# Expert pairs planned one segment early, weights shared by two tiles in three buffers, and start-up transfers in the order of their use

## The reference, cut to what matters

```
mod = (silu(c) @ wmod).reshape(4, 6, 1, -1)
sa, ca, ga, sb, cb, gb = mod[:, 0], ..., mod[:, 5]
ga = (2 * (ga >= 0) - 1) * maximum(abs(ga), 0.25)     # gb the same way
h = layernorm(x) * (1 + ca) + sa
x = x + ga * attention(h)
h = layernorm(x) * (1 + cb) + sb
x = x + gb * ffn(h)
```

```
h = gelu(tokens @ W1[e] + b1[e]);  out[e] = h @ W2[e] + b2[e]
out = weight_1 * out[first expert] + weight_2 * out[second expert]
```

## Time and profile before

| | |
|---|---|
| median of 3 runs | 3398.45 us (3397.02 to 3399.81) |
| the profiled execution's own time | 3402.84 us |
| its span, first to last instruction | 3401.1 us |
| mean granted TensorE clock | 0.832 |
| PE / DVE / ACT / POOL busy | 77% / 52% / 35% / 18% |
| HBM traffic | 211.41 MB read, 53.76 MB written |

### The profile page before, as it was taken

How to read it: one execution, slowest core, us unless ns; L and a number is a source line. 1 busy time by engine, 2 the same in 40 slices (tenths; PEclk the granted TensorE clock), 3 DMA queues, 4 the chain that set the end, 5 groups by cost and what they waited for, 6 DMA issues and landing times.

```text
span 3401.1 us, 78002 instructions
## 1 busy us (share of the span) xinstructions
PE 2615.6 (77%) x33890; PEld 1936.5 (57%) x33890; DVE 1759.1 (52%) x3974; ACT 1202.0 (35%) x2396; POOL 609.8 (18%) x621
## 2 busy tenths in 40 slices
PE   3458878877896888788787969886687646779998
PEld 3244556456645655575466456555544546668887
DVE  4554766485658556765856585566439421111111
ACT  0322454255326333642553263335125412212221
POOL 0003300600060034006100600340010011102222
PEclk8667987888697979768986979797688768889999
DMA  2122201411130132013112301320110067667665
GB/s 78 32 64 57 51 2 55 103 20 45 49 77 9 45 76 57 2 46 100 33 45 50 76 9 45 75 51 2 57 63 2 7 206 235 207 232 213 199 202 152
DMA packets 230150, 266.00 MB, mean 78 GB/s; under 512 B 148064, under 2 KB 175600, under 8 KB 227440
## 3 DMA queue, kind: packets, MB, share of 16 engines
q1 hardware_dynamic: 214464, 234.79, 24.0%
q0 software_dynamic: 15344, 26.22, 3.2%
HBM read 211.41 MB, written 53.76 MB: 78 GB/s over the span
## 4 chain that ended last, share of the span: by engine, by line
PE 57%; DVE 19%; ACT 9%; DMA 7%; issue 5%; SPq 2%; POOL 0%; DVEq 0%; ACTq 0%
PE banks L1964 19%; DMA arena<-in_cols 6%; PE banks L2489 6%; PE banks L2508 4%; PE banks L2279 4%; PE banks L2196 3%; PE banks L2299 2%; PE banks L2304 2%; DVE hT L1530 2%; PE banks L2231 2%; PE banks L2066 1%; PE banks L2038 1%; PE banks L2107 1%; ACT arena L895 1%; ACT ring L895 1%
## 5 line engine op out<-in xcount | busy, mean ns | idle before, releaser
L2489 PE MATMUL banks<-arena 128*128 128x256 f32 (+1 forms) x1472 | 282.8, 357 | 88.3 <-DMA arena<-in_cols 88.2
L1873 POOL DMA_INDIRECT h_d<-h_tok,pos_now x64 | 66.0, 1031 | 1453.4 <-DVE pos_now L1715 1436.4
L2489 PEld LDWEIGHTS banks<-arena 128*128 128x128 f32 x1472 | 252.0, 213 | 120.0 <-DMA arena<-in_cols 98.0
L1082 ACT ACTIVATE arena<-banks,arena 128x256 f32<-128x256 f32 (+1 forms) x368 | 136.3, 421 | 520.3 <-PE banks L2489 520.3
L1964 PE MATMUL banks<-hT,ring 128*128 128x512 f32 x640 | 297.8, 622 | 7.8 <-DVE arena L1380 7.8
L2279 PE MATMUL banks<-arena 32*32 32x64 f32 (+2 forms) x6144 | 185.6, 294 | 144.5 <-ACT arena L906 64.5
L2279 PEld LDWEIGHTS banks<-arena 32*32 32x32 f32 (+2 forms) x6144 | 165.0, 175 | 182.2 <-issue 103.3
L2508 PE MATMUL banks<-arena 128*128 128x256 f32 x1136 | 252.6, 379 | 0.0
L2279 PE MATMUL banks<-arena,xn 32*32 32x64 f32 (+2 forms) x6144 | 166.3, 289 | 109.8 <-DVE xn L1538 58.6
L1964 PE MATMUL banks<-arena,ring 128*128 128x512 f32 x512 | 224.0, 595 | 6.2 <-ACT arena L852 6.2
L2508 PEld LDWEIGHTS banks<-arena 128*128 128x128 f32 x1136 | 212.4, 190 | 27.1
(11 more groups left out here) (364 smaller groups left out, 4827.6 us busy)
## 6 DMA issues: line engine op xcount, KB each, us to landing
arena<-in_w_ring SPq DMA_DIRECT2D x92, 1024.0 KB, 7.3
ring<-in_w_ring SPq DMA_DIRECT2D x104, 512.0 KB, 4.3
arena<-h_d SPq DMA_DIRECT2D x25, 516.0 KB, 4.0
n_d<-NA SPq DMA_DIRECT2D x8, 1024.0 KB, 3.9
arena<-n_d SPq DMA_DIRECT2D x16, 512.0 KB, 8.1
u_d<-arena SPq DMA_DIRECT2D x8, 1024.0 KB, 3.9
NA<-u_d SPq DMA_DIRECT2D x32, 256.0 KB, 5.6
arena<-in_b SPq DMA_DIRECT2D x46, 128.0 KB, 8.0
```

Source lines behind the costliest of these rows:

```text
L1082: ins_ = act.activation(hid1[:, i % 2, t, 0:SPAN[i] * P], bank[pair][:, half * T1:half * T1 + SPAN[i] * P], ACT.Gelu, bias=b1[:, i % 2, t: ...
L2489: i_ = mm(bank[t // 2][:, (t % 2) * T1:(t % 2) * T1 + n], w1[:, i % 2, t // 4, at_:at_ + P], h_cols[:, i % 2, k, 0:n], start=(k == 0), sto ...
```

## The change

Four things change together.

1. **Start-up in order of use.** SP issues the condition vector, the part of `wmod` for the first shift and scale, and `x` first, then what turn -2 needs, then the rest of `wmod`, then everything else; four semaphores (`first_in`, `pre_in`, `mod_in`, `tables_in`) take the place of one, and `started` is gone. The gates and columns, still the same products, are made inside turn -2, between the projections; the small tables inside turn -1. Gate tiles share banks (`MOD_BANK`), so three of the eight products wait for DVE to have read an earlier one (`gates_ok`).
2. **Pairs.** The expert stage still has 46 tiles, but the lists are 9 pairs of 512 rows (two full tiles that load their weights once), 7 single full tiles and 21 halves: 37 groups with loads of their own. `AFTER` mixes the halves between the pairs and singles; three full tiles end the list, behind the copy to the output.
3. **Early pairs.** Seven pairs are certain to be filled by the first seven segments alone. They are planned in turn 7 (`plan_ahead`), and the first two tiles' transposes, first products and gelu are done in turn 7. The other lists are planned behind it (`plan_rest`, on DVE within tile 0).
4. **Three buffers.** Weights have three buffers (`WBUF`), taken from arrays that are free by then.

```diff
-SEQ = [FULLS + n for n in range(HALVES)] + list(range(FULLS))
+LISTS = ((EARLY1, 2 * T1), (TWICE - EARLY1, 2 * T1), (SINGLE, T1), (HALVES, P))
+AFTER = (0, 0, 2, 2, 2, 2, 3, 3, 3, 1, 1, 1, 1, 0, 0, 0)
+TILES = [(g, part) for g, slot in enumerate(GROUPS) for part in range(2 if slot < TWICE else 1)]
+WBUF = 3
...
+            sp.dma_start(c_cols, ins["c_cols"]).then_inc(*up16(first_in))
+            sp.dma_start(wmod[0][:, :, 0:2 * D], ins["wmod"][0][:, :, 0:2 * D]).then_inc(*up16(first_in))
+            sp.dma_start(X_next, x_seg[0:1].rearrange("a p b d -> (a p) b d")).then_inc(*up16(x_next_in))
+            sp.dma_start(consts[:, 0:m0], ins["consts"][:, 0:m0]).then_inc(*up16(pre_in))
+            for t, name in ((w_qkv, "w_qkv"), (cols, "cols"), (w_beta, "w_beta")):
+                sp.dma_start(t[:], ins[name]).then_inc(*up16(pre_in))
+            sp.dma_start(wmod[0][:, :, 2 * D:], ins["wmod"][0][:, :, 2 * D:]).then_inc(*up16(mod_in))
+            sp.dma_start(wmod[1], ins["wmod"][1]).then_inc(*up16(mod_in))
...
+                if rest and not nxt:
+                    sp.wait_ge(plan_ok.handle, 1)
+                    sp.wait_ge(h_out.handle, h_out.base(seg))
+                    load_w1(0)
+                    for i in range(2):
+                        load_rows(i)
+                    load_w2(0)
...
-            sp.wait_ge(started.handle, 4 * TURNS + 4)
+            for g in range(1, WBUF):
+                load_w1(g)
+                if g == 1:
+                    for i in range(2, ROWBUF):
+                        load_rows(i)
+                load_w2(g)
+            sp.wait_ge(plan_ok.handle, 2)
             sp.wait_ge(h_out.handle, h_out.base(NSEG))
...
+            for i, (g, _) in enumerate(TILES):
+                if i:
                     sp.wait_ge(y_ok.handle, i)
+                if i + ROWBUF - 1 == SPAN.index(1):
+                    sp.wait_ge(zero_out.handle, 16 * (E1 + 1))
+                if i and i + ROWBUF - 1 < NTILES:
+                    load_rows(i + ROWBUF - 1)
+                if i and ENDS[i - 1] and TILES[i - 1][0] + WBUF < TILES1:
+                    load_w2(TILES[i - 1][0] + WBUF)
...
+                if ENDS[i] and g + WBUF < TILES1:
                     sp.wait_ge(hid1_ok.handle, 4 * (i + 1))
+                    load_w1(g + WBUF)
...
                     if pre:
                         next_norm()
+                    if not nxt:
+                        plan_ahead()
                     for hg in range(HG):
                         state_step(hg)
                     residual(2, (0, 1), 1, 0, "b_out")
+                    if not nxt:
+                        for i in range(2):
+                            columns(i)
                     layer_norm(3)
...
                 if rest:
                     norm_root(3)
+                    if not nxt:
+                        gelu_tile(0)
...
                 if rest:
                     norm_modulate(3, 1, 2)
+                    if not nxt:
+                        gelu_tile(1)
```

More of the change, by code:

```diff
@@ new lines, in plan_rest @@
+            def plan_rest():
+                plan_step(dve.tensor_copy(pad_i[0:1, :], next_row[0:1, :]))
+                plan_step(dve.memset(zeros, 0.0))
+                plan_step(dve.tensor_scalar(zeros[:, TOKEN:TOKEN + 1].bitcast(I32), token_no[:, 0:1], float(B * L), None, ALU.add))
+                plan_step(dve.scalar_tensor_tensor(left, begin, -1.0, next_row[:, :], ALU.mult, ALU.add))
+                plan_step(dve.memset(jump, float(E1 * REGION)))
+                slot = LISTS[0][0]
+                for (n, size), most in zip(LISTS[1:], MOST[1:]):
+                    assign(slot, n, size, most)
+                    slot += n
+                dve.sem_inc(*up(plan_ok))
@@ L1881, in turn @@
                 counted(seg, [zeroed, sub_step] if nxt or not rest else [zeroed])
-                if nxt or not rest:
-                    pool.sem_inc(started.handle, 1)
             turns(turn)
@@ new lines, in hidden @@
+            def hidden(i):
+                n = SPAN[i] * P
+                g = TILES[i][0]
+                pe.wait_ge(w1_in[g % WBUF].handle, 32 * (g // WBUF + 1))
+                pe.wait_ge(cols_ok.handle, i + 1)
+                for t in range(HT1):
+                    if i and t % 2 == 0:
+                        pe.wait_ge(hid1_ok.handle, 4 * (i - 1) + t // 2 + 1)
+                    for k in range(KC):
+                        at_ = k * SLOT // KC + t % 4 * P
+                        i_ = mm(bank[2 + t // 2][:, (t % 2) * T1:(t % 2) * T1 + n], w1[g % WBUF][:, t // 4, at_:at_ + P],
+                                h_cols[:, i % 2, k, 0:n], start=(k == 0), stop=(k == KC - 1))
+                    if t % 2:
+                        i_.then_inc(*up(h1_mm))
@@ L2364, in turn @@
                     delta_rows(range(quarter))
-                if pre:
+                if pre and rest:
                     project(0, 0)
@@ L2378, in turn @@
                     turn_rows(3)
-                if pre:
+                    if not nxt:
+                        hidden(1)
+                if pre and rest:
                     for k in range(KC):
                         project(1, k)
+                if seg == PRE:
+                    mod_gates((5, 6, 7))
                 if nxt:
@@ L2405, in turn @@
                         project(2, k)
+                if seg == PRE:
+                    pe.wait_ge(emb_sq.handle, 1)
+                    for k in range(KC):
+                        i_ = mm(bank[1][:, 64:64 + E1], const("ones"), esq[:, k], start=(k == 0), stop=(k == KC - 1))
+                    i_.then_inc(emb_sum.handle, 1)
                 def turn_tokens(j):
```

617 lines of the change are left out of this document (321 added, 296 removed).

## The result

| | before | after |
|---|---|---|
| median | 3399.13 us of 4 runs (3397.02 to 3416.17) | 3198.97 us of 4 runs (3192.26 to 3210.06) |
| profiled execution, its span | 3402.84, 3401.1 us | 3210.06, 3208.2 us |
| mean granted clock | 0.832 | 0.838 |
| HBM read | 211.41 MB | 191.32 MB |

What follows compares the result with a forecast made beforehand. Bounds: a serial start, PE idle behind turn 7, and halves asking for weights too late. Savings of 151.6 us (seam, stage, end) and 42.2 (start) took 3402.84 to 3209.0; the median forecast was 3205 us, range 3174 to 3256.

Steps and rivals of the forecast that it cites:

- The theory: Expert stage: halves wait because weights are asked for too late with two buffers; waits and slow clock cost 119.6 us.
- The rival of the halves that go on waiting: Expert stage: transfers land as late as before, each half keeps losing 4.7 us, giving 3297 us; chance 0.13.
- The term for waits left in the stage: Expert stage: PE's remaining waits with three buffers, taken as 6 us between bounds of nothing and 27.
- 494.9 us of PE: Expert stage: PE time for all tiles without waits, 509.8 us less 14.9 already done in turn 7.
- The routing was forecast 3.6 us later: Turn 7's end: early tiles make routing end at 2725.5 instead of 2721.86; bounds 0 and 7 us.
- The loss to the clock behind it: Behind turn 7's routing: fallen clock slows a first product, 2.8 us, bounds 0 and 5.
- The zero rows were to cost 5: Early expert stage: nine zero rows in SP's queue delay tile 4's rows, 5 us, bounds 0 and 10.
- the two convolutions (52.9 and 69.5): Turn -2: forecast starts of DVE's second and third convolutions, the second 50.4 us earlier than before.
- the gram product (86.2): Start: first product of turn -1 at 86.2 us against 128.43, so 42.2 us less.
- the prediction's 16 for even sharing: Start: with engines shared evenly among all issued transfers, the first two come near 16 us; the start gains about 37.
- 14.7 us were forecast from PE's end to the span's end: End: the old 11.7 us plus 3 for POOL adding three tiles one behind the other, bounds 0 to 6.
- The rival of slow adds: Expert stage: POOL adds tile by tile, waiting for each landing; 15.3 us per tile would undo everything; chance 0.02.

Runs made afterwards that it cites:

- e1: Changed kernel with two weight buffers in place of three; median 3300.45 us, 0.9709 of the kernel before.
- e2: Changed kernel, but the second tile of every pair but the first loads its weights again (45 loads, not 37); median 3202.41 us, ratio to before 0.9413.
- e11: Changed kernel with both two weight buffers and own weights for the second tile of each pair but the first; median 3339.89 us, ratio to before 0.9801.
- e4: Changed kernel with the nine zero rows issued behind the rows of tile 4, not ahead; median 3189.87 us, ratio to before 0.9373.
- e7: Changed kernel with the first two tiles' transposes, first products and gelu moved behind turn 7; median 3208.42 us, ratio to before 0.9430.
- e8: As e7, with the early pairs also planned and their weights asked for behind turn 7; median 3230.58 us, ratio to before 0.9483.
- e5: Changed kernel, but ACT's first instruction waits until every transfer of the start has landed; median 3213.13 us, ratio to before 0.9438.
- e9: Changed kernel with all gate and column products ahead of turn -2's first projections, transfers still in order of use; median 3192.98 us, ratio to before 0.9369.
- e6: Changed kernel with turn -2's second projections ahead of the 24 column products, not behind; median 3189.66 us, ratio to before 0.9360.

## Why the prediction was right, point by point

**The halves.** The theory was that they were bound neither by PE nor by the rate, but by asking too late. e1 and e2 tell that apart: the buffer is worth 103 us, the eight loads 2 to 4 with three buffers (40 with two, e11). The rival of the halves that go on waiting was priced at 3297; e1, which brings its waits back, has 3300. The term for waits left in the stage was 6 us; two waits and 3.2 us were measured. Its base, 494.9 us of PE, holds: 507.9 less 3.2 of waits, 8.3 at the rows of tile 4, 1.0 of slower first product and 0.7 of gap leaves 494.7.

**The seam.** The routing was forecast 3.6 us later; it is 4.9 (2.38 of it a wait for DVE's column copy, which was to lie within the first `hidden`). The loss to the clock behind it was to be 2.8; the first product has 8.05 us for 7.07, so 1.0. The zero rows were to cost 5, with a bound of 10: 6.40 of wait and 1.9 of slower products are 8.3, and e4 takes back 8.9. The mechanism was named rightly, its size was set too low: the wait was 1.4 us longer, and the slower products behind it were left out. By e7 and e8 the early tiles bring 10.7 us, and the plan and loads in turn 7 another 23.2, of which up to 7.3 are e8's wait for the last segment's rows.

**The start.** The steps came out at 16.27 for `mod_in` (16.2 forecast), 25.8 for the end of the first projections (27.0), 48.9 and 65.9 for the two convolutions (52.9 and 69.5), 83.6 for the gram product (86.2). The first projections took 3.60 us, not 6.50, at the full clock. The sum took the edit as a whole and did not say which part of it brings the gain. By e5 the order of the transfers is 14.8 us. The other 30 us are not the interleaving, since e9 undoes it and is 5.6 us shorter. From the rows they are the early `x`, normalized ahead of the gate products, gate steps on DVE that run beside PE's products, where before each stood behind the other, and the small tables, for which DVE needed about 5 us between its last gate step and the load of `x` and which now lie in turn -1; no run tried these parts one by one. By e6 the size of the interleaving was misjudged: the columns were priced by their time before (10.3 us; 5.28 in e6), and the wait for DVE was taken as given, while another order of the same products is 8.7 us shorter.

By the Trainium skill (DMA: Bandwidth & Descriptors, Queues, rings and completion order) a DMA engine takes one queue's descriptors in the order of issue, and the first transfers were to land near 5 us. The trace agrees, though the first function, at 5.60, does not show it: by then SP had issued nine of the 28 transfers, so the prediction's 16 for even sharing, which counts all of them, was no fair rival. What shows it are the small ones: the 8 KB of the condition vector, first in the queue, landed 1.8 us after their issue, the 16 KB of `w_beta`, issued at 4.13 behind 2.1 MB, only after 6.0 us.

**The end.** 14.7 us were forecast from PE's end to the span's end, 12.7 were measured. The rival of slow adds needed a landing of 15.3 us; the page of the changed kernel has a median of 7.3, for 7.4 before, beside 222 GB/s moved in all:

```profile
acc_d<-arena,S POOLq DMA_INDIRECT x65, 7.3
```

**The sum.** The spans differ by 192.9 where 193.8 was forecast, but errors cancel in this: start, stage and end gained 6.1 us more than forecast (2.7, 1.4 and 2.0), turn 7's end lost 1.3 more, and the turns between took 5.8 more with their code unchanged. That is a spread between executions (below): the profiled execution of the changed kernel has the longest turns of the thirteen profiles, and is the slowest of its four runs. The median, at 3198.97, is 6 us below the 3205 forecast.

## What to carry to other kernels

When a stage waits for transfers at two thirds of the DMA engines' share, ask first when each load is issued: one buffer more was worth 103 us here, eight loads fewer 2 to 4 (40 with one buffer less). Whatever the queue issues or waits for ahead of a load counts as its latency (the zero rows, the adds ahead of the copy, the last segment's rows). And work that is moved between other steps is not hidden by that alone: the gates and columns between the projections made the start 5.6 us longer than in one piece, and moving the columns alone made it 8.7 us shorter. Look at what each piece puts off, and at the clock that it meets.

## What was not expected of the hardware

- The same column products took 9.83 us at a granted clock of 0.52 behind small logits products, with PE busy all the time, and 5.28 us at 1.00 behind projections of 128x512 (e6). Where a step stands sets its price by a factor of nearly two. The granted clock that the profile shows does not always tell: the first 16 of these records, at 5.96, took 3.54 us, 0.22 us each, as slow as at 0.52, under a shown clock of 1.00, and so did the 64 of the kernel before, in 13.79 us. No run tells why.
- The turns between, whose instructions are the same in the twelve kernels that have the change (but for a plan moved in e8), took from 2544.7 to 2565.5 us in their profiles: 0.8%. A gain of 9 us is not seen in one execution's time, but plainly in the stage that it changes. What makes the spread was not tried.
- SP took 9.27 us to issue eight zero rows whose addresses come from registers, 1.16 us each.
